# Mamba scan with attention and experts: the B rows broadcast in one fp32 product, a shorter Newton step, and a normalisation placed later

## The reference

```python
def _forward(x, W_in, conv_w, conv_b, W_x, A_log, D_param, W_dt, b_dt, W_out):
    xz = x @ W_in.T
    x_ssm, z = jnp.split(xz, 2, axis=-1)
    ...
    x_ssm = jax.nn.silu(jnp.transpose(xc, (0, 2, 1)))
    proj = x_ssm @ W_x.T
    B_ssm = proj[..., :D_STATE]
    C_ssm = proj[..., D_STATE:2 * D_STATE]
    dt = jax.nn.softplus(proj[..., -1:] * W_dt[:, 0] + b_dt)
    A = -jnp.exp(A_log)
    def step(h, inp):
        dt_t, Bt, Ct, xt = inp
        dA = jnp.exp(dt_t[..., None] * A)
        h = dA * h + (xt * dt_t)[..., None] * Bt[:, None, :]
        y = jnp.einsum('bdn,bn->bd', h, Ct)
        return (h, y)
    ...
    y = jnp.transpose(ys, (1, 0, 2)) + x_ssm * D_param
    y = y * jax.nn.silu(z)
    return y @ W_out.T
x = _layernorm(x + _L0_attn_ref(x, ...), axis=-1)
x = _layernorm(x + _L0_xattn_ref(x, ctx_1024, ...), axis=-1)
x = _layernorm(x + _L0_ffn_ref(x, ...), axis=-1)
```

## Time and profile before

| | us |
|---|---|
| median of 3 runs | 1689.43 |
| lowest and highest run | 1685.65, 1699.95 |
| the profiled execution, its own time | 1687.66 |
| span of that execution in the trace | 1685.9 |

### The profile page before, as it was taken

The page is one execution under the profiler, slowest core; times in us unless marked ns, Lnnn a source line. Parts: engine busy times, 40 slices in busy tenths (PEclk is TensorE's granted clock), DMA queues, the critical chain, the costliest instruction groups (busy, mean ns, idle before and its releaser), DMA issues. The chain is left out here.

```text
span 1685.9 us, 22891 instructions
## 1 busy us (share of the span) xinstructions
PE 1361.7 (81%) x7612; PEld 959.2 (57%) x7612; DVE 1466.5 (87%) x2714; ACT 1113.7 (66%) x2452; POOL 902.0 (54%) x659
## 2 busy tenths in 40 slices
PE   7687778778877877787877879988998899889880
PEld 5566566656666666566665645456545654464460
DVE  5999999999999999999999956597859785978678
ACT  5877887788788778877887523337633763375570
POOL 1778877787878788788778600002800280028015
PEclk9889889888988998998898989999999999999995
DMA  7200210221022022102111021100020001000000
GB/s 237 67 26 32 69 68 3 70 70 42 28 70 70 1 69 70 58 13 70 64 33 56 13 86 46 40 1 1 11 70 1 1 14 38 1 1 1 25 1 25
DMA packets 38040, 70.02 MB, mean 42 GB/s; under 512 B 3553, under 2 KB 31682, under 8 KB 33698
## 3 DMA queue, kind: packets, MB, share of 16 engines
q1 hardware_dynamic: 37922, 68.56, 12.1%
HBM read 59.90 MB, written 8.65 MB: 41 GB/s over the span
## 5 line engine op out<-in xcount | busy, mean ns | idle before, releaser
L900 POOL TENSOR_TENSOR state_c<-state,c_area 128x1024 f32<-128x1024 f32 x256 | 601.7, 2361 | 168.2 <-DVE state L970 149.0
L970 DVE TENSOR_TENSOR_SCAN state<-decay,ps 128x512 f32<-128x512 f32 x512 | 620.5, 1212 | 0.0
L686 ACT ACTIVATE decay<-step_area,negA 128x255 f32<-128x255 f32 x1024 | 432.5, 496 | 0.5 <-DVE step_area L1049 0.5
L945 DVE TENSOR_TENSOR ps<-step_area,ps 128x512 f32<-128x512 f32 x512 | 349.7, 683 | 10.6 <-PE ps L368 8.5
L1562 POOL TENSOR_TENSOR big<-big,g_sb 128x1024 f32<-128x1024 f32 x29 | 80.8, 2788 | 504.8 <-ACT big L1462 502.8
L384 PE MATMUL ps<-ident_sb,state_c 128*128 128x128 f32 x2048 | 294.8, 292 | 12.6 <-POOL state_c L900 12.5
L384 PEld LDWEIGHTS ps<-ident_sb,state_c 128*128 128x128 f32 x2048 | 255.5, 151 | 40.7 <-POOL state_c L900 23.0
L368 PE MATMUL ps<-parts,sel_bc_sb 96*128 96x256 bf16 x256 | 75.4, 295 | 95.8 <-DVE ps L961 75.8
L1421 PE MATMUL ps<-w_sb,hT 128*128 128x256 f32 x512 | 119.9, 388 | 2.4 <-ACT hT L1531 1.9
L1386 PE MATMUL ps<-w_sb,weights 128*128 128x512 f32 x256 | 121.0, 608 | 0.1
L1650 DVE BATCH_NORM_STATS2 stats<-big 128x6 f32<-128x256 f32 x256 | 88.4, 414 | 28.1 <-ACT big L1536 20.2
(11 more groups left out here) (210 smaller groups left out, 2386.6 us busy)
## 6 DMA issues: line engine op xcount, KB each, us to landing
c_area<-c_scratch SPq DMA_DIRECT2D x32, 1024.0 KB, 6.4
weights<-in_xT SPq DMA_DIRECT2D x16, 256.0 KB, 3.0
res<-in_x SPq DMA_DIRECT2D x16, 256.0 KB, 2.8
x_scratch<-res SPq DMA_DIRECT2D x16, 256.0 KB, 8.2
weights<-x_scratch SPq DMA_DIRECT2D x4, 1024.0 KB, 7.8
xa<-x_scratch SPq DMA_DIRECT2D x4, 1024.0 KB, 5.4
out_x<-acc SPq DMA_DIRECT2D x4, 1024.0 KB, 4.4
w_sb<-in_w SPq DMA_DIRECT2D x2, 1024.0 KB, 13.8
```

The source lines that it names most:

```text
L686: nc.scalar.activation(decay[:, n % RING, j, 1:], dt_sb[:, i[1] % 2, j, 1:], ACT.Exp, scale=negA[:, j * NS + n:j * NS + n + 1]).then_inc(s ...
L900: nc.gpsimd.tensor_tensor(state_c[:, n % RING, :, :], state[:, n % RING, :, :], c_bc[:, q, n, :].unsqueeze(1).to_broadcast([P, CT, TC]), A ...
L945: nc.vector.tensor_tensor(bu_ps[m % 3][:, :].rearrange("p (j n) -> p j n", j=2), u_sb[:, i[1] % 2, 2 * h:2 * h + 2, :], b_ps[n % 2][:, 0:T ...
L970: nc.vector.tensor_tensor_scan(state[:, n % RING, pair, :].rearrange("p j n -> p (j n)"), decay[:, n % RING, pair, :].rearrange("p j n -> ...
```

## The change

The bf16 split is gone: `project` gives 33 rows (16 of B, 16 of C, one of dt), ACT copies them once, and `b_row` is one fp32 product of the 16 B rows with a column of the identity, repeated 128 times by a zero step. `step_row` uses the identity's column 32 the same way, in place of `sel_p`. The loads of `sel_bc` and `sel_p` go. POOL's constants become immediates: the mean and the variance are one tensor_scalar each, and the Newton step has five operations where it had six. ACT's `spreads` move from place 3 to 5, `guess` from 6 to 8, `normalise` from 9 to 13; POOL's `variance` from 2 to 3 and `newton` from 4 to 6.

```diff
-PROJ = PARTS * BC + 1
+PROJ = BC + 1
...
             def step_row(k):
-                pe.wait_ge(s_projc, at(k, 2, 2))
-                nc.tensor.matmul(w_ps[:, 0:TC], sel_p_sb[:, :], proj[:, k[1] % 2, :], start=True, stop=True)\
+                pe.wait_ge(s_projc, at(k, 1, 1))
+                nc.tensor.matmul(w_ps[:, 0:TC], ident_sb[0:PROJ, BC:PROJ].to_broadcast([PROJ, P]), proj[:, k[1] % 2, :], start=True, stop=True)\
                   .then_inc(s_step, 1)
...
             def b_row(i, n):
                 if n == 0:
-                    pe.wait_ge(s_split, at(i, 2, 2))
+                    pe.wait_ge(s_projc, at(i, 1, 1))
                 pe.wait_ge(s_bu, at(i, 4 * NS, 4 * n + 4))
-                nc.tensor.matmul(b_ps[n % 2][:, 0:TC], sel_bc_sb[:, n, :], parts[:, i[1] % 2, :], start=True, stop=True)\
+                nc.tensor.matmul(b_ps[n % 2][:, 0:TC], ident_sb[0:NS, n:n + 1].to_broadcast([NS, P]), proj[0:NS, i[1] % 2, :],
+                                 start=True, stop=True)\
                   .then_inc(s_b, 1)
...
                 nc.scalar.activation(proj[:, k[1] % 2, :], w_ps[0:PROJ, 0:TC], ACT.Copy).then_inc(s_projc, 1)
-                nc.scalar.activation(lead[:, :], w_ps[0:PARTS * BC, 0:TC], ACT.Identity,
-                                     scale=par_sb[0:PARTS * BC, MASKS:MASKS + 1]).then_inc(s_projc, 1)
...
-                    work += [(0, lambda: take_sum(old, 0)), (1, lambda: take_sum(old, 1)), (3, lambda: spreads(old)), (6, lambda: guess(old)),
-                             (9, lambda: normalise(old))]
+                    work += [(0, lambda: take_sum(old, 0)), (1, lambda: take_sum(old, 1)), (5, lambda: spreads(old)), (8, lambda: guess(old)),
+                             (13, lambda: normalise(old))]
...
-                nc.gpsimd.tensor_tensor(var[:, :], spread[:, :], per_dm, ALU.mult).then_inc(s_mv, 1)
-                pool.wait_ge(s_mv, at(k, 2, 2))
-                nc.gpsimd.tensor_tensor(var[:, :], var[:, :], eps, ALU.add).then_inc(s_nw, 1)
+                nc.gpsimd.tensor_scalar(var[:, :], spread[:, :], 1.0 / DM, LN_EPS, ALU.mult, ALU.add).then_inc(s_nw, 1)
...
-                nc.gpsimd.tensor_tensor(newt[:, :], newt[:, :], half, ALU.mult).then_inc(s_nw, 1)
-                pool.wait_ge(s_nw, at(k, 7, 4))
-                nc.gpsimd.tensor_tensor(newt[:, :], one_half, newt[:, :], ALU.subtract).then_inc(s_nw, 1)
-                pool.wait_ge(s_nw, at(k, 7, 5))
+                nc.gpsimd.tensor_scalar(newt[:, :], newt[:, :], -0.5, 1.5, ALU.mult, ALU.add).then_inc(s_nw, 1)
+                pool.wait_ge(s_nw, at(k, 6, 4))
...
-                    work += [(0, lambda: centre(old)), (2, lambda: variance(old)), (4, lambda: newton(old))]
+                    work += [(0, lambda: centre(old)), (3, lambda: variance(old)), (6, lambda: newton(old))]
                 if prepare:
-                    work += [(8, lambda: split(k, 0)), (10, lambda: make_dt(k)), (10, lambda: first_arg(k)),
-                             (10, lambda: split(k, 1)), (11, lambda: make_u(k)),
+                    work += [(10, lambda: make_dt(k)), (10, lambda: first_arg(k)),
+                             (11, lambda: make_u(k)),
                              (12, lambda: injections(k, 0, NS - RING))]
```

More of the change, by code:

```diff
@@ L43, with mamba_block @@
 TG = 4
-def mamba_block(nc, x, xT, w_in, w_x, w_out, par, ident_sb, ident, sel_bc, sel_p, c_dram, x1, ahead, s_ahead, ps, early, late, shared,
+def mamba_block(nc, x, xT, w_in, w_x, w_out, par, ident_sb, ident, c_dram, x1, ahead, s_ahead, ps, early, late, shared,
                 w, ctxT):
@@ L622, in first_decay @@
                 nc.scalar.activation(first_dA[:, k[1] % 2, :, :], first_dA[:, k[1] % 2, :, :], ACT.Exp).then_inc(s_dA, 1)
-            def next_lead(k):
-                act.wait_ge(s_split, at(k, 2, 1))
-                nc.scalar.activation(lead[:, :], rest[:, :], ACT.Identity,
-                                     scale=par_sb[0:PARTS * BC, MASKS + 1:MASKS + 2]).then_inc(s_lead, 1)
             def terms(k, j):
@@ L742, in turn @@
                              (12, lambda: terms(k, 0)), (12, lambda: terms(k, 1)), (12, lambda: terms(k, 2)),
-                             (12, lambda: terms(k, 3)), (12, lambda: softplus(k)),
-                             (13, lambda: next_lead(k))]
+                             (12, lambda: terms(k, 3)), (12, lambda: softplus(k))]
                 if finish:
@@ L862, in centre @@
                 pool.wait_ge(s_r, at(k, CTT, 3 * CTT))
-                nc.gpsimd.tensor_tensor(mean[:, :], total[:, :], minus_per_dm, ALU.mult).then_inc(s_mv, 1)
+                nc.gpsimd.tensor_scalar(mean[:, :], total[:, :], -1.0 / DM, None, ALU.mult).then_inc(s_mv, 1)
             def newton(k):
@@ L907, in _ @@
             nc.gpsimd.memset(decay[:, :, :, 0], 0.0).then_inc(s_zero, 1)
-            for c, value in enumerate((0.5, 1.5, 1.0 / DM, LN_EPS, -1.0 / DM)):
-                nc.gpsimd.memset(coef[:, c, :], value).then_inc(s_coef, 1)
-            half, one_half, per_dm, eps, minus_per_dm = (coef[:, c, :] for c in range(5))
             pool.sem_inc(s_sum, RING)
@@ L1915, in decoder_block @@
             ahead.append((w[name][tuple(slice(None) for _ in shape)], source))
-        mamba_block(nc, x, xT, w_in, w_x, w_out, par, ident_sb, ident, sel_bc, sel_p, c_dram, x1, ahead, s_ahead, ps, early, late,
+        mamba_block(nc, x, xT, w_in, w_x, w_out, par, ident_sb, ident, c_dram, x1, ahead, s_ahead, ps, early, late,
                     shared, w, ctxT)
@@ L1921, in _constants @@
 def _constants():
-    one = 0x3F80
-    sel_bc = np.zeros((PARTS * BC, NS, P), np.uint16)
-    for q in range(PARTS):
-        for n in range(NS):
-            sel_bc[BC * q + n, n, :] = one
-    sel_p = np.zeros((PROJ, P), np.float32)
-    sel_p[PROJ - 1] = 1
     before = np.tri(E, k=-1, dtype=np.float32).reshape(E * E)
-    return dict(ident=np.eye(P, dtype=np.float32), sel_bc=sel_bc, sel_p=sel_p, before=before)
+    return dict(ident=np.eye(P, dtype=np.float32), before=before)
 def _layout(inputs):
@@ L1950, in _layout @@
     par = np.zeros((P, PAR_COLS), f32)
[L1951 removed]
+    par[:, :] = np.concatenate([per_channel(attn(n)) for n in
                                          ("A_log", "conv_w", "conv_b", "D_param", "W_dt", "b_dt")], 1)
[L1953 to L1954 removed]
     w_x = attn("W_x").T
```

63 lines of the change are left out of this document (14 added, 49 removed).

## The result

| | before | changed |
|---|---|---|
| median of 4 runs of each, us | 1694.69 | 1737.47 |
| lowest and highest, us | 1685.65, 1700.82 | 1734.00, 1739.01 |
| span of the profiled execution, us | 1685.9 | 1735.8 |

The ratio is 1.0265, with a 95% interval of 1.0233 to 1.0298: slower by 2.7%.

The account below looks back on a forecast made before the run. DVE was taken to bound the first block. First rows +2.8, preparing chains -2.3, mid-turn waits -0.8 and last turn -1.4 gave -1.7 us: 1686.0 against the profiled 1687.7, stated as 1687, range 1677 to 1702.

Parts of the forecast that it names:

- signs of being wrong: New mid-turn waits of DVE before products, a B row's load well over 0.2 us, or scans not lasting 1212 ns.
- the place to watch: First B row of a turn, just in time for DVE: its shift goes to the time in nine to eleven turns.
- The price of a row: B row on PE: an fp32 pair takes 0.43 us, 0.32 more than bf16; 0.64 more at the slow clock.
- My upper bound: Cost of a B row on PE: at most 0.64 us more, in every place; lower bound 0.
- On average it is hidden: PE idles 12.2 us per turn and 16 dearer rows take 5.1 of it, so outside the stall's wake they cost nothing.
- -0.23 us for ACT: ACT up to take_y_back: 0.98 - 0.36 - 0.39 - 0.46, so PE's stall ends 0.23 us earlier.
- The 0.36 and 0.46 us: ACT's gains ahead of take_y_back: 0.36 from dropping `lead`, at most 0.46 from normalise leaving place 9.
- The credit of 2.3 us for late preparing chains: With ACT's spreads at place 5, the stall ends earlier in about five turns, 0.45 us each on average: -2.3.
- The clock: Related to the all-waits-gone rival: more passes per row could hold PE's clock faster; given no chance of its own.
- The last turn: PE starts up to 2.5 us earlier with spreads behind POOL's mean; 1.4 taken off DVE's two waits of 2.7 us.
- The start: Two loads fewer before the first scan, but none was waited for on the way: gain 0.
- the wake gets longer: Rival: stall ends 0.23 us later, first row 1.2 later in all 15 turns, 1706 (chance 0.05); half, 1697 (0.12).

Follow-up runs that it names:

- e3: Changed kernel with a real 16 x 128 0/1 matrix per state in place of the repeated identity column; 1739.93 us, ratio 1.0301.
- e1: Changed kernel with the B row and step row over 128 rows, zero-padded, still fp32; 1684.83 us, ratio 0.9962.
- e4: Changed kernel with the norm's steps back at their old places (ACT 3, 6, 9; POOL 2, 4); 1730.49 us, ratio 1.0238.
- e15: Kernel before with four useless 128x256 fp32 products put in PE's stall; 1694.29 us, ratio 1.0007.
- e7: Changed kernel with project padded to 64 columns, B rows and step row over 64 partitions; 1726.47 us, ratio 1.0178.
- e14: Changed kernel with four useless 128x256 fp32 products ahead of state 14's row, behind add_state of place 12; 1701.90 us, ratio 1.0073.
- e13: e1 with only the two rows behind PE's stall (states 15 and 0) over 16 rows, the others over 128; 1694.54 us, ratio 1.0009.

## Why the prediction was wrong

The range of 1677 to 1702 missed by 35 us. I had forecast no difference that can be told, and the kernel is 2.7% slower. Of my signs of being wrong one came: a new wait of DVE inside a turn, 2.16 us at 926.49, beside the 52.5 us of idle where I had said 4 to 12. And a row held PE for 0.62 us instead of 0.43.

*Right:* the first block goes at DVE's pace, and the place to watch was the first row of a turn behind PE's stall; a shift of it did go to the time in 11 of 14 turns. DVE's own work is the same. The stall stayed, 13 times and up to 3.2 us; ACT's wait for POOL's mean went; `add_state` no longer waits for POOL there. The zero step costs nothing (194 ns; e3).

*The price of a row* was the first step that failed. I took 0.43 us from start to start of a 128-row fp32 pair and called the row 0.32 us dearer than the bf16 one. For 128 rows that is what it costs (317.11 to 317.54 in e1), but the new row has 16. At a turn's start the time from `out_tile`'s last pair to `add_state` went from 0.54 us (317.91 to 318.45) to 1.14 (390.89 to 392.03): 0.6 dearer. Behind the stall the gap from row to `add_state` went from 0.71, POOL's wait included, to 1.15. My upper bound (0.64 in every place) held the size, but I summed it over the two rows of the wake only. I wrote that going from 96 rows to 16 gives nothing back. It takes something.

*"On average it is hidden"* was the second. Fourteen rows a turn lie before the stall, and PE's 12.2 us of idle did not hide them: PE is late at `project`, and ACT with it by 1.0 us. I had worked out -0.23 us for ACT; it is +1.57: this 1.0, and 0.57 from `normalise` ahead of `take_y_back` less `next_lead` (0.98 - 0.39). The 0.36 and 0.46 us that I credited at places 9 and 11 were swallowed, since ACT waits for PE there: its copy of z's second product stands 1.08 us for PE in the turn of 449.85, and stood not at all in that of 433.90. The credit of 2.3 us for late preparing chains never came; e4, without the new places, is 7 us faster.

*The clock* was the largest, and I gave it no chance of its own. With the stall filled, 35 of the 43 us are back without touching a gap, though 12 of them in the last turn, where nothing was filled. (Wide rows take back all of it with the stalls left in, so the two causes are not two shares of a sum.) The price of the slow clock is plain in the earlier trace rows (four transposes 1.11 us against 0.63), but I only saw it as a factor on two rows, not on the 9 us of path that stand behind the stall. What the gaps did was to bring DVE to the point where that path is no longer covered. In the kernel before the slow wake is there too (6.44 us on average over 15 turns from the second `y_back` to the next turn's first row, 5.32 in e15), and costs nothing that e15 could win back.

*The last turn* was forecast at -1.4 us and came to +11.2 in DVE's waits (13.97 against 2.73). What the runs show in its place is the slow clock for 28 us. The 64-row rows of e7 have the same gaps but not this spell, so the gaps alone do not make it; what brings it on is open.

*The start:* forecast 0, and +1.15 between the two traces (the first scan at 31.31 against 30.16). It is not the change: ACT's first copy of the convolution, ahead of every narrow product, already starts 1.17 us later (16.14 against 14.97), and in e3, with the same narrow products, the first scan starts at 30.07.

*The rivals:* "the wake gets longer" was the right one. It asked for a shift of over 1.1 us in every turn; the turns are 2.3 us longer on average (60.6 against 58.3), and the last one 13, so even its 1706 was too low. Its reasons were not the measured ones: the 0.23 us of ACT and 0.96 of PE that it adds up hold neither the gaps of the fourteen rows in mid-turn nor the slow clock over the rest of the path.

Open: why the slow clock lasts for the whole path (502 to 510) with both kinds of narrow rows, and in most turns ends sooner with either kind alone. The gaps leave PE idle in short pieces there, but no run separates these from the length and phase of the stall. Of the 16 us between the traces of e14 and e1, 3.3 are lost ahead of turn 2 (it starts at 143.72 in e14 and at 140.45 in e1), a wait of 5.45 us stands at 900.02, and about 6 lie in the second block, which is the same code in both.

## What to carry to other kernels

Price a product as it stands between its neighbours: here one over 64 rows or fewer among products over 128 cost up to 0.33 us of idle on each side, and padding it with zero rows took the loss away. Where an engine's stall stands ahead of a path that another engine waits for, look at the granted clock behind the stall, and price the whole path at it. Before moving an instruction into a gap, ask what copy it was covering. And where two kernels differ in one block, compare that block in the traces: from DVE's first L978 (L1020 before) on, this program took 697.7 us in the trace of e1 and 702.5 in that of before, with the same code.

## What the hardware showed that was not expected

- 0.33 us of idle before the weight load of a row over 16 or 64 rows in fp32, or 32 in bf16, at full clock; behind the fp32 rows again 0.33 us before the next load, behind the bf16 row 0.12. None at 97 or 128 rows.
- At the slow clock the row and its gap took 1.15 us (503.44 to 504.59), against 0.85 for a 128-row pair in e1.
- Four useless products per turn, with `add_state` moved ahead of the row, went with a changed kernel 35 us faster.
- PE stayed at the slow clock for 28 us while it was busy for 25.9 of them (949 to 977), in a last turn that in other kernels with narrow rows (e7, e13, e14) had no such spell.
- In the kernel before, a stall of 2.30 us was followed by the slow clock (484.88); in e14 stalls of 1.2 to 2.3 us were not. The stall is not all that differs: before, PE had also stood 1.96 us ahead of the row at 481.42, and in e14 the filler stands there.
